# A fused attention and mixture-of-experts block: fewer row buffers, gathers issued five tiles ahead, and output stores moved to the loading queue

## The reference, cut to what matters

```python
x = _layernorm(x + _L0_attn_ref(x, ...), axis=-1)
x = _layernorm(x + _L0_ffn_ref(x, ...), axis=-1)
```

```python
buf = zeros((E, CAP + 1, H)).at[se, slot].set(x[tok])[:, :CAP]
h = silu(einsum('ech,ehf->ecf', buf, w_gate)) * einsum('ech,ehf->ecf', buf, w_up)
out = einsum('ecf,efh->ech', h, w_down)
gathered = out[se, minimum(pos, CAP - 1)] * valid[:, None]
y = segment_sum(gathered * w, tok, num_segments=Tn)
shared = silu(x @ ws_gate) * (x @ ws_up) @ ws_down
return y + shared
```

## Time and profile before

| | us |
|---|---|
| median of three runs | 1337.28 |
| profiled execution, whole | 1344.97 |
| its span | 1343.1 |
| attention and first shared units, until the first gather | 1205.9 |
| first scatter starts | 1232.38 |
| last scatter starts | 1299.72 |
| TensorE busy | 1296.6 (97%) |

### The profile page before, as it was taken

The page is one execution under the profiler, slowest core; times in us unless marked ns, Lnnn a source line. Parts: engine busy times, 40 slices in busy tenths (PEclk is TensorE's granted clock), DMA queues, the critical chain, the costliest instruction groups (busy, mean ns, idle before and its releaser), DMA issues.

```text
span 1343.1 us, 39655 instructions
## 1 busy us (share of the span) xinstructions
PE 1296.6 (97%) x15292; PEld 1102.8 (82%) x15292; DVE 1031.0 (77%) x2344; ACT 922.9 (69%) x1738; POOL 482.0 (36%) x413
## 2 busy tenths in 40 slices
PE   7999999999999999999999999999999999997985
PEld 5788888888888888888888888888888888873564
DVE  6677879787878788787978787878878797874426
ACT  7667777777767777777777777777777777732425
POOL 0224243324233333424332423333342433335754
PEclk9999999999999999999999999999999999998998
DMA  8700000000000000000000000000000004486968
GB/s 305 261 2 10 28 9 21 15 1 27 9 27 10 27 9 27 10 27 9 24 13 1 27 9 27 18 27 17 27 18 27 17 19 126 133 265 160 237 109 314
DMA packets 48607, 82.17 MB, mean 61 GB/s; under 512 B 4849, under 2 KB 30545, under 8 KB 47569
## 3 DMA queue, kind: packets, MB, share of 16 engines
q1 hardware_dynamic: 39376, 66.64, 15.0%
q0 software_dynamic: 4608, 7.08, 3.0%
q10 hardware_dynamic: 4480, 6.29, 1.3%
HBM read 57.31 MB, written 22.69 MB: 60 GB/s over the span
## 4 chain that ended last, share of the span: by engine, by line
PE 85%; DMA 5%; DVE 4%; issue 2%; ACT 2%; SPq 1%; POOL 1%; DVEq 0%; ACTq 0%; POOLq 0%
PE pA L613 25%; PE pB L613 24%; PE pO L712 12%; PE pC L698 10%; PE pS L675 10%; DMA sums<-sb_stage,sb_sidx 3%; PE pC L613 1%; DMA sb_W<-sums 1%; DMA sb_stage<-wprep 1%; DVE sb_W L1253 1%; SPq L604 1%; ACT sb_W L969 1%; PE pB L897 1%; PE pC L737 1%; SPq L600 0%
## 5 line engine op out<-in xcount | busy, mean ns | idle before, releaser
L1758 POOL TENSOR_TENSOR sb_vl<-sb_v,sb_vh 128x512 f16<-128x512 f32 x121 | 154.2, 1274 | 680.2 <-ACT sb_vh L1015 680.2
L613 PE MATMUL pB<-sb_xh,sb_W 128*128 128x256 f16 x2048 | 350.4, 273 | 0.6 <-ACT sb_kh L997 0.5
L1304 DVE TENSOR_TENSOR sb_S<-pS,sb_D 128x1024 f32<-128x1024 f32 x248 | 235.9, 952 | 120.3 <-PE pS L675 120.3
L1023 ACT ACTIVATE sb_Shl<-sb_S 128x1024 f16<-128x1024 f32 x242 | 204.3, 844 | 110.7 <-DVE sb_S L1304 109.3
L613 PE MATMUL pB<-sb_xl,sb_W 128*128 128x256 f16 x1024 | 279.7, 273 | 0.0
L1310 DVE TENSOR_TENSOR sb_Shl<-sb_S,sb_Shl 128x1536 f16<-128x1536 f32 x121 | 225.3, 1862 | 10.5 <-ACT sb_Shl L1023 10.4
L613 PEld LDWEIGHTS pB<-sb_xh,sb_W 128*128 128x128 f16 x2048 | 200.3, 99 | 23.8 <-DVE sb_W L1253 0.8
L613 PE MATMUL pA<-sb_xh,sb_W 128*128 128x256 f16 x1024 | 175.8, 274 | 10.0 <-DVE sb_W L1253 5.6
L613 PE MATMUL pA<-sb_W,sb_xh 128*128 128x256 f16 x1024 | 175.9, 274 | 2.6 <-ACT sb_qh L990 2.6
L712 PE MATMUL pO<-sb_Wo,sb_yh 128*128 128x256 f16 x1016 | 173.3, 273 | 0.0
L1029 ACT ACTIVATE sb_gt<-pB 128x512 f32<-128x512 f32 x128 | 76.5, 598 | 140.4 <-PE pB L613 140.4
(11 more groups left out here) (361 smaller groups left out, 2700.9 us busy)
## 6 DMA issues: line engine op xcount, KB each, us to landing
sb_stage<-wprep SPq DMA_DIRECT2D x7, 1280.0 KB, 6.3
sb_W<-w_experts SPq DMA_DIRECT2D x17, 384.0 KB, 3.8
gather_rows<-sb_xr SPq DMA_DIRECT2D x16, 320.0 KB, 2.4
sb_W<-sums SPq DMA_DIRECT2D x10, 512.0 KB, 13.6
sb_xs<-xT SPq DMA_DIRECT2D x16, 256.0 KB, 2.9
sb_D<-decay SPq DMA_DIRECT2D x8, 512.0 KB, 7.5
sb_xn<-x SPq DMA_DIRECT2D x16, 256.0 KB, 3.1
sums<-sb_xr SPq DMA_DIRECT2D x16, 256.0 KB, 2.2
```

The source lines that it names most:

```text
L613: last = nc.tensor.matmul(dst, a, m, start=(i == 0), stop=(i == len(terms) - 1), **kw)
L1023: nc.scalar.activation(Sh[:, :, a:z_], S[:, :, a:z_], ACT.Copy).then_inc(s_Sh, 1)
L1304: nc.vector.tensor_tensor(scores_at(h)[:, :, a:z_], pS[:, :, a:z_], d[:, :, 0:z_ - a], ALU.mult).then_inc(s_Sm, 1)
L1758: nc.gpsimd.tensor_tensor(vl[q % 2][:, :, :], v32[:, :, :], vh[q % 2][:, :, :], ALU.subtract).then_inc(s_vl, 1)
```

## The change

It has four parts. (1) The ring of gathered rows has 8 buffers instead of 12, all in the staging buffer; the buffers that had held four of them (`y32`, `sq`, `xn`, `z`) are left alone. Five gathers are issued ahead instead of 12. (2) There are four output row buffers instead of six; the space goes to the transposed tokens of the unmixed tiles, which had been in `x1T`, so that ScalarE's first copy no longer waits for the last use of `x1T`. (3) GpSimd adds the regions of six chunks (1, 2, 3, 5, 6, 7) instead of four, VectorE of two (0, 4) instead of four, and three chunks instead of six are loaded region by region. (4) The output stores are issued by SyncE behind all loads of the sums, instead of by ScalarE, each behind its chunk.

```diff
-XRING = 12
-AHEAD = 12
+XRING = 8
+AHEAD = 5
-OUTBUF = 6
+OUTBUF = 4
-BY_POOL = (1, 3, 5, 7)
-SPLIT = 6
+BY_POOL = (1, 2, 3, 5, 6, 7)
+SPLIT = 3
-        in_stage = carve(P, XRING - 4, ROW)
-        xg = [in_stage[:, r, :] for r in range(XRING - 4)] + [a[:, 0:ROW] for a in (y32, sq)]
-        xg += [a[:, :, :].rearrange("p t n -> p (t n)")[:, 0:ROW] for a in (xn, z)]
+        in_stage = carve(P, XRING, ROW)
+        xg = [in_stage[:, r, :] for r in range(XRING)]
         wo = carve(P, OUTBUF, HID)
-        xgT = [x1T[:, t, :] for t in range(NC)] + [v32[:, t, :] for t in range(NT)]
+        xgT = carve(P, NC, NC * P)
+        xgT = [xgT[:, t, :] for t in range(NC)] + [v32[:, t, :] for t in range(NT)]
@@ sync
                 sp.dma_start(fin[c], regions[c]).then_inc(s_fl[c], 16)
+            for n, c in enumerate(ORDER):
+                sp.wait_ge(s_fo, n + 1)
+                sp.dma_start(out_t[c], fin[c][:, 1, :, :]).then_inc(s_out, 16)
@@ scalar
-                if t == 0:
-                    act.wait_ge(s_x1l, SEQS)
...
-                act.wait_ge(s_fo, n + 1)
-                act.dma_start(out_t[c], fin[c][:, 1, :, :]).then_inc(s_out, 16)
```

## The result

The changed kernel takes 1395.77 us (median of three runs, 1393.64 to 1396.32) against 1337.28: the ratio is 1.0424, with a 95% interval of 1.0408 to 1.044. It is 58.5 us slower. I had predicted 1375, at most 1393.

The account below looks back on a forecast made before the run. TensorE was taken to set the pace in the expert tiles, one tile per 2.7 us. Tiles +42, burst -4, clock +2 and end -2 gave +38 us on 1337.28: 1375 us, range 1355 to 1393.

Parts of the forecast that it names:

- The gather wait: Transposes from tile 6 on wait for gathers queued behind scatters: a path of 3.24 + 3.6 + 0.62 = 7.5 us.
- the low end: Smallest slowdown for five gathers ahead in the tiles: 5.9 + 8 x 8.5 + 11 = 84.9 us, +26 us.
- the chain: In the expert tiles, merge, copy, scatter, gather, then transpose waiting; two interleaved chains, odd and even tiles, share TensorE.
- two tiles take 7.5 + 2.7: In the expert tiles, one wait path plus one TensorE step per two tiles: 10.2 us, 5.1 us per tile.
- the clock at +2 us: TensorE's clock dropping as it idles in the tiles: +2 us, or some +14 if mostly at 1.2 GHz.
- W: Time from the copy of tile 0's merged rows to the end of tile 23's copy: 59.1 us before, +42 forecast.
- half clock: Rival: the waits keep TensorE at 1.2 GHz through most of the tiles, +38 + 12, 1387 us; chance 0.11.
- The tail: From tile 22's transpose to the end of tile 23's copy: 14.5 us before, 12 taken.
- The shorter burst, -4 us: Ahead of tile 0's rows, six first gathers instead of 13 free the engines sooner: -4 us, from -8 to 0.
- Buffers, 0 us: Four output buffers and eight row buffers cost 0 us in the tiles while gathers set the pace; otherwise about +4.
- The end, -2 us: From tile 23's copy to the end, with moved adds and stores: 50.6 against 52.85 us, from -6 to +3.

Follow-up runs that it names:

- The filler: The changed kernel plus 30 unused matmuls on TensorE ahead of each wait for the gathers of tiles 6, 8, ... 22: 1383.54 us, ratio 1.0333.

## Why the prediction was wrong

The direction, the place and the wait held. The time was missed by 20.8 us and lies 3 us outside the range. By its own steps:

- **The gather wait: the path was right.** The changed kernel has nine waiting transposes (tiles 6 to 22). From the copy of tile 0 (1225.33) to the transpose of tile 22 (1327.34) it is 102 us. TensorE's steps in between take 36.8 us; the rest over 9 is 7.25 us for each wait path. I had predicted 7.5 from the earlier trace rows (and 5.9 for the low end, where its terms give 6.0). The gathers took 3.1 to 4.7 us to land where I had taken 3.6, and the reaction behind it is 0.14 us, not the 0.62 that I took from a row of another place. The Trainium skill has a fit (DMA: Bandwidth & Descriptors, Anatomy of one DMA, SWDGE path): 2.0 us plus bytes over 436 GB/s. An estimate by it for 163,840 B is 2.4 us, and the trace disagrees: no gather on the chain landed in under 3.09 us.
- **The step that failed: "two tiles take 7.5 + 2.7", with the clock at +2 us.** The eight steps that the chain passes (tiles 6 to 20) took 4.03 to 5.10 us, 4.60 on average, where I had 2.7. That is 8 x 1.9 = 15.2 us more than my sum, and with the shorter path (-2.2) 13.0 us, against the 2 us that I had given the clock. I had seen the cause, and had priced it at up to 14 us, yet took 2: I argued from TensorE's busy share over the whole stretch. The order in time decides. Behind each idle stretch the clock is down (0.50 to 0.67 in these steps), and the step there is on the path. The filler shows it on the same chain: clock 0.97, and from the transpose of tile 6 to that of tile 22 it is 83.6 us in place of 94.7, which is 11 us back; W is shorter by 10.1 and the time by 12.2. The rival "half clock" had the right cause, and with 1387 us it too was below the measured time. The clock's term should have come from a row of before, the stretch at 0.65, in place of a guess.
- **The tail: 12 us taken, 15.2 measured.** From the transpose of tile 22 to the end of tile 23's copy I had taken 2.5 us off the 14.5 of before, for waits on late scatters that would not recur. Only 0.9 us of it went. TensorE waits three times there for VectorE's part of the same tile, in both kernels (the first of the three waits, before and now; all three are 1.11, 1.00 and 1.19 us before and 0.89, 1.00 and 0.96 now):

```profile
1284.43 0.41 PE L917 MATMUL pS<-sb_W,sb_qh 96*32 96x256 f32 x2 [1.11 <-DVE sb_ql L1692]
```

```profile
1337.42 0.41 PE L920 MATMUL pS<-sb_W,sb_qh 96*32 96x256 f32 x2 [0.89 <-DVE sb_ql L1691]
```

  The stretch from these waits on is 0.9 us shorter than before (6.0 against 6.9 us), and the one ahead of them 1.6 us longer (9.2 against 7.6), where the step behind tile 22's wait again ran at a low clock (0.68, against 1.00 before):

```profile
1275.75:1277.90 2.15, 2.15 (x32) 1.07 (x31) 0.86 (x3) 1.00 (x4) 1.55 (x1) 1.00 0.60 65
```

```profile
1327.34:1330.47 3.13, 3.13 (x30) 1.16 (x31) 0.34 (x3) 1.44 (x5) 0.95 (x1) 0.68 0.58 94
```

  Together 13.0 + 3.2 = 16.2, and 42 + 16.2 = 58.2: the measured +58.1.
- **The shorter burst, -4 us: there in the profiles, not in the comparison.** The stretch fell from 25.2 to 17.2 us. But the profiled execution before took 1344.97 us and the timed runs 1337.22 to 1339.1, a difference of the same 8 us. That the timed runs lack the long stretch is inferred, since they have no trace; the second profile of that kernel speaks for it, with 18.7 us there at 1341.43. I had carried "the profiled execution is 7.7 us above the median" through as a constant and also booked a gain for a part of it. With the term at 0 the sum would have been 42 - 2 + 2 = 42.
- **Buffers, 0 us: right at five ahead** (the distance alone costs as much as the whole change). With twelve ahead four output buffers cost 3.8 us, near the 4 that I had named for a kernel whose pace the gathers don't set.
- **The end, -2 us: the size is met (-1.7), the reason is not shown.** The statistics of the second chunk came 23.7 us behind W (22.6 predicted), the norm took 21.2 (22.1), the rest 6.2 (5.9). But the kernel with five ahead and the old end has 50.8 us from W to the end, less than the 51.1 here. So what I had put down to the edits of the end came without them, and that the number fits is luck.

On this reading what was missed is 14.1 us in W (58.1 for 42 + 2), 4 for the burst, 2.2 ahead of the first gather and 0.3 at the end, 20.6 of 20.8 us.

What was only argued and not shown: that in the held stretch of the earlier trace rows the row of gathers itself is what holds the engines. Five profiled executions had all thirteen in a row; four of them had 24.9 to 25.8 us there and one 18.7, and what differs in that one is open. Six had five to eight ahead, with 16.6 to 18.0 us. The two with the first gathers spread out had 20.2 and 20.3, so that the spread gave 4.6 us and not the 8. Open as well is where the rest of W's excess at seven and eight ahead (12 and 8 us) comes from: four output buffers alone, with twelve ahead, made W 5.9 us longer.

## What to carry to other kernels

Count the distance of a prefetch in the steps of the engine that waits, and compare it with the whole path: end of the work that opens the slot, the slot itself, landing, reaction. Here the path is 7.25 us and a step 2.7, and with this queue order the waits were nearly gone only at seven ahead. The last step taken away, from six to five ahead, cost 36 us in W. When a wait of some us returns in a loop, price the work behind it at the lower clock as well, because that work is on the path. And before a stall that the profile shows is booked as a gain, see whether the timed runs contain it: an offset between the profiled execution and the median is the place to look.

## What the runs showed of the hardware

- Matmuls without a use in an idle stretch made the kernel faster: 30 with a result of 96x256 in f16 before every second tile, clock 0.74 to 0.97, 1395.8 to 1383.5 us.
- The same 47 or 48 TensorE instructions took 2.85 us at a granted clock of 1.00 and 4.65 at 0.61; with filler the steps were long in the two places where the clock was low (4.38 us at 0.61, 4.29 at 0.60).
- A gather of 128 rows of 1280 bytes landed 3.1 to 3.3 us after its issue with the DMA engines 0.54 to 0.57 busy, and 3.9 to 4.7 us after it with them 0.88 to 1.00 busy.
- With 13 indirect gathers issued in a row it took 24.9 to 25.8 us from the first of them to the first result in four executions and 18.7 in a fifth; with five to eight ahead it took 16.6 to 18.0. In one of the four the clock was 0.50 over 14 us; with six in a row and the others spread, at the same data rate, it was 0.77, and 4.6 us came back.
